# A signal of its own for the gate half of the products in the expert tiles

## What is computed

```python
x = x + tanh(g_xattn) * mlstm(layernorm(x), ctx, ctx)        # 16 heads, over 128 positions
h_in = layernorm(x)                                           # 1024 x 256
logits = 30 * tanh(h_in @ w_gate / 30)                        # 8 experts
weights = softmax(logits) * (one of the 2 largest)
for e in range(8):
    h = silu(h_in @ w1[e]) * (h_in @ w3[e])                   # 256 -> 512
    out += h @ w2[e] * weights[:, e:e+1]                      # 512 -> 256
x = x + tanh(g_ffn) * out
```

## Time and profile before

| | us |
|---|---|
| median of the 3 runs | 222.68 |
| lowest and highest run | 222.11, 222.68 |
| span of the profiled execution | 219.9 |
| PE busy in the span | 200.4 (91%) |
| VectorE (DVE) busy | 161.1 (73%) |
| ScalarE (ACT) busy | 140.4 (64%) |
| GpSimd (POOL) busy | 89.4 (41%) |

### The profile page before, as it was taken

One profiled execution on the slowest core, in us unless ns is written; L12 is line 12 of the kernel. 1 busy time (PEld: TensorE's weight loads), 2 busy tenths in 40 slices (PEclk: granted clock), 3 DMA queues, 4 the chain that ended last, 5 costly groups with the idle time before them and its releaser, 6 DMA issues.

```text
span 219.9 us, 4347 instructions
## 1 busy us (share of the span) xinstructions
PE 200.4 (91%) x1373; PEld 142.2 (65%) x1374; DVE 161.1 (73%) x354; ACT 140.4 (64%) x281; POOL 89.4 (41%) x96
## 2 busy tenths in 40 slices
PE   8999899989889898979999999999999999999930
PEld 3478554434346544468888888888888888888720
DVE  6897764688989889998777747767767777667520
ACT  2387878898964797746666645566566665665510
POOL 8100254338380000611555555555444555532232
PEclk9999999999999999999999999999999999999996
DMA  3999999921010124110222332334333233342212
GB/s 110 322 366 375 372 375 372 373 88 48 3 48 3 48 87 156 48 51 24 51 48 48 51 48 48 52 51 67 56 54 60 48 48 48 53 62 33 24 24 24
DMA packets 20034, 23.43 MB, mean 107 GB/s; under 512 B 3888, under 2 KB 15152, under 8 KB 20016
## 3 DMA queue, kind: packets, MB, share of 16 engines
q1 hardware_dynamic: 13696, 16.94, 22.4%
q0 software_dynamic: 4464, 6.16, 17.1%
q10 hardware_dynamic: 1856, 0.10, 0.6%
HBM read 17.95 MB, written 5.24 MB: 105 GB/s over the span
## 4 chain that ended last, share of the span: by engine, by line
PE 67%; DVE 16%; ACT 6%; DMA 4%; issue 3%; POOL 1%; DVEq 0%; ACTq 0%; POOLq 0%
PE bank L1446 28%; PE bank L1258 7%; PE bank L1466 6%; PE bank L1478 6%; PE bank L1457 5%; PE bank L1298 3%; PE bank L1469 3%; DMA x_sb<-in_x_dram 3%; ACT arena L511 2%; PE bank L1428 2%; DVE w_sb_r L973 2%; DMA out_dram<-hraw,sidx 2%; PE bank L1274 2%; PE bank L1179 1%; DVE st L801 1%
## 5 line engine op out<-in xcount | busy, mean ns | idle before, releaser
L1446 PE MATMUL bank<-arena_r,xn_sb_r 128*128 x176 | 54.6, 391 | 0.0
L471 POOL DMA_INDIRECT out_dram<-hraw,sidx x16 | 26.1, 1632 | 38.5 <-DVE hraw L1135 22.5
L1446 PEld LDWEIGHTS bank<-arena_r,xn_sb_r 128*128 128x128 f32 x176 | 33.1, 188 | 6.7
L1446 PE MATMUL bank<-w_sb_r,xn_sb_r 128*128 x88 | 36.5, 415 | 0.3 <-issue 0.2
L676 ACT ACTIVATE x_sb<-bank 128x512 f32<-128x512 f32 x23 | 13.8, 599 | 29.7 <-PE bank L1446 26.4
L432 POOL TENSOR_SCALAR_AFFINE_SELECT arena<-arena 128x1024 f32<-128x1024 f32 x16 | 17.6, 1102 | 36.5 <-ACT arena L541 36.5
L1086 DVE TENSOR_TENSOR x_sb<-x_sb,bank 128x512 f32<-128x512 f32 x23 | 15.8, 686 | 16.4 <-ACT x_sb L676 16.4
L1162 PE MATMUL bank<-ones_b 128*128 128x512 bf16 x103 | 25.6, 397 | 1.1 <-POOL ones_b L385 1.1
L454 POOL DMA_INDIRECT cvT<-xnorm_scratch,gidx x12 | 12.3, 1028 | 31.2 <-DVE gidx L1035 23.4
L851 DVE TENSOR_TENSOR arena<-bank,arena 128x1024 f32<-128x1024 f32 x16 | 19.5, 1222 | 6.8 <-POOL arena L432 6.6
L973 DVE TENSOR_TENSOR w_sb_r<-w_sb,arena_r 128x512 fp32r<-128x512 f32 x32 | 20.1, 683 | 0.1
(11 more groups left out here) (234 smaller groups left out, 403.9 us busy)
## 6 DMA issues: line engine op xcount, KB each, us to landing
w_sb<-in_L_ffn_w_dram SPq DMA_DIRECT2D x24, 512.0 KB, 9.4
x_sb<-in_x_dram SPq DMA_DIRECT2D x2, 512.0 KB, 6.7
arena<-in_ctx_dram SPq DMA_DIRECT2D x2, 512.0 KB, 9.3
out_dram<-x_sb SPq DMA_DIRECT2D x8, 128.0 KB, 1.8
xnorm_scratch<-xn_sb SPq DMA_DIRECT2D x8, 128.0 KB, 1.9
out_dram<-hraw,sidx POOLq DMA_INDIRECT x16, 3.8
cvT<-xnorm_scratch,gidx POOLq DMA_INDIRECT x12, 2.8
hraw<-xnorm_scratch,gidx POOLq DMA_INDIRECT x11, 2.8
```

The costliest lines, as they stand in the source:

```text
L471: nc.gpsimd.indirect_dma_start(out=out[:, :], out_offset=bass.IndirectOffsetOnAxis(ap=sidx[:, i:i + 1], axis=0), in_=y_sb[i % YBUF], in_of ...
L1446: last = nc.tensor.matmul(ps_scores[p][:, n, :], a, w, start=(k == 0 and j == 0), stop=(k == KC - 1 and j == 2))
```

## The change

The signal `s_gu` becomes two. `s_gt` is raised by the last matmul of the gate half, `s_gu` by the last of the up half, as before. `silu` waits for `s_gt` alone; `hidden` waits for the SiLU and for `s_gu`. In `first_gate_up` the signals stand at the last gate and the last up matmul of its second part. No instruction is added, removed or moved on any engine: what differs is which semaphore an instruction raises or waits for, 23 more signals on PE and one more condition on each of the 23 `hidden` instructions.

```diff
-        s_gu = sem("gate_up_done")
+        s_gt = sem("gate_done")
+        s_gu = sem("gate_and_up_done")
...
             def silu(i, p):
-                act.wait_ge(s_gu, i + 1)
+                act.wait_ge(s_gt, i + 1)
...
             def hidden(i, p):
                 dve.wait_ge(s_si, i + 1)
+                dve.wait_ge(s_gu, i + 1)
                 nc.vector.tensor_tensor(h_sb[p], sg_sb[p], ps_scores[p][:, 1, :], ALU.mult).then_inc(s_hm, 1)
...
             def gate_up(i, p, e, split=True):
...
                             last = nc.tensor.matmul(ps_scores[p][:, n, :], a, w, start=(k == 0 and j == 0),
                                                     stop=(k == KC - 1 and j == 2))
-                last.then_inc(s_gu, 1)
+                    last.then_inc((s_gt, s_gu)[n], 1)
...
             def first_gate_up():
...
                                                         stop=(lower == 1 and k == KC - 1), skip_group_check=True)
-                last.then_inc(s_gu, 1)
+                        if lower:
+                            last.then_inc((s_gt, s_gu)[n], 1)
```

## The result

| | before | changed |
|---|---|---|
| median of 11 runs, us | 222.09 | 220.88 |
| lowest run, us | 221.79 | 220.50 |
| span of the profiled execution, us | 219.9 | 218.7 |

The changed kernel takes 0.9942 of the time before (95% interval 0.9928 to 0.9957): 1.2 us less by the medians, 1.3 by the ratio. One run of each kernel, 224.39 and 224.44 us, lies far above the others; without them the medians are 222.05 and 220.87. The span fell by 1.2 us, from 219.9 to 218.7; 218.8 was forecast. The sum of the change was right, and the time it was taken from was not.

The account below looks back on a forecast made before the run. PE's chain was taken to bound the kernel; 0.8 us from the loop's gaps and 0.3 from the last step give 1.1 to 1.15 off 219.9, to 218.8. Plus 2.8 outside the span: 221.5 us, range 221.0 to 222.5.

Parts of the forecast that it names:

- What bounds: Expert tiles: the chain runs along PE alone, so only its standing still or its matmuls stretching can win or lose time.
- SiLU and `hidden` earlier: Step 9 into 10: SiLU starts near 142.02 instead of 142.99, `hidden` near 142.98, 0.64 us earlier, with 0.62 us margin.
- The 11 gaps: Before `turn_h` in steps 9 to 19: 0.07 to 0.08 us each vanish, 0.8 us less, bounds 0 and 0.9.
- The last step: Before `gate_up(22)`: the stall from a late register load behind `turn_h(21)` goes, 0.32 us less, bounds 0 and 0.36.
- The end: Last addition waits for the DMA of tile 21, not for tile 22: earlier `turn_h(22)` worth 0, at most 0.2 us.
- the start: `hidden(0)` starts when `split(1)` lets go of DVE, and steps 1 to 7 have no gap before `turn_h`: worth 0.
- the signals: Extra signals on PE and waits on DVE: 0, at most 0.01 us per signal and 0.2 us for 23.
- Signals that cost: Signals amid the twelve `gate_up` matmuls hold the next by up to 0.03 us: 0.6 us given back, 222.1; chance 0.08.
- a stretch by SiLU's reads: SiLU reading the gate bank stretches the up half's six matmuls; at 20 ns each 2.8 us, 224.3 in all; chance 0.05.
- The unmoved gap: The loop's gap is PE's own register work and stays; only the final step gains, 222.4 us; chance 0.14.
- a gain in the loop only: The register load before `gate_up(22)` may wait for the transposes, so that stall stays: 221.9 us; chance 0.10.
- idle that moves elsewhere: Nothing happens, as PE's idle moves, for one to the wait for `lower_x`: 222.6 us; chance 0.05.

Follow-up runs that it names:

- the loop alone: The changed kernel with SiLU waiting for the gate half alone only in tiles 8 to 18, elsewhere for the up half: 221.24 us, 0.9960 of the time before.
- tile 21 alone: The changed kernel with SiLU waiting for the gate half alone only in tile 21, elsewhere for the up half: 221.72 us, 0.9972 of the time before.
- its own experiment: The kernel before, with only the register load of the last tile's expert moved ahead of `turn_h(21)` on PE: 221.64 us, 0.9978 of the time before.
- the late SiLU: The kernel before, with SiLU of tiles 8 to 18 also waiting for the two transposes behind `gate_up`: 225.02 us, 1.0125 of the time before.

## Why the prediction was right, and where it was wrong

**What bounds.** Right: PE alone, and the two kinds of stall named from "issue" waits were all that the change touched on it. **SiLU and `hidden` earlier**: `hidden` at 142.99 for 142.98 forecast. SiLU started at 141.85, earlier than the 142.02 forecast: the step began 0.07 us sooner by the closed gap, and ACT's row of SiLU begins 0.09 us before that of `upper_w2` ends (140.79 + 1.15). The reserve is 0.55 us instead of 0.62. The hit on `hidden` to a hundredth was luck in part: everything stood 0.07 us sooner, and the product came 0.11 us behind the end of `gate_up` where 0.03 was reckoned with. The lead of SiLU over the end of `gate_up`, put at 0.97 us, was 0.93 by the prediction's own rows (142.95 less 142.02) and came out at 1.03.

**The 11 gaps.** 0.8 us forecast; 0.82 in the chain, and 0.9 to 1.0 by the runs of the loop alone. **The last step.** 0.32 forecast within 0 to 0.36; with steps 20 and 21 the chain has 0.40, and 0.34 with tile 21 alone. The cause given, the register load, is shown by its own experiment. **The end, the start, the signals.** 0 each, and so they came out, but for 0.10 us by which one addition landed later. "No instruction is added" was wrong by 23, at no cost that can be measured.

**The step that failed** is the last of the sum: "The median of the runs stands 2.8 us over that span, the lowest 2.2. Kept at 2.8, this gives 221.5 us." The profiled execution was taken for a typical one of the three runs, and all the difference for time outside the span (2.2 to 2.8 us, as the section on the time before has it too). The runs that list both show 1.7 to 1.8 us outside the span in every single one, before as changed (220.51 with a span of 218.7). So the execution with a span of 219.9 was one of about 221.7 us, faster than all eleven runs, and the three first lay high: their median is 222.68, that of the eleven 222.09. The span forecast, 218.8, and 1.8 outside would be 220.6 us, and the forecast difference, 1.15 us, taken from the median of the eleven 220.94, both close to the 220.88 measured. The range failed by the same term: its low end, 221.0, is the span forecast with the 2.2 us of the fastest of the three runs, when 1.8 was the true term.

**The rivals.** Signals that cost and a stretch by SiLU's reads are out: `gate_up` has 2.75 to 2.78 us with SiLU reading beside it, 2.75 to 2.79 before. The unmoved gap is out by the list of waits and by the late SiLU; a gain in the loop only, by the run of tile 21 alone; idle that moves elsewhere, by the chain, where PE has no new wait.

## What to carry to other kernels

On an engine that the profile shows busy all the time (PE for 49.05 us of the 49.05 in ten loop steps before) the gain can lie in gaps of 0.1 us at one place of each step: look for weight loads that wait for "issue" and compare their start with the end of the work that they depend on. A consumer that needs half of a product gets a signal at that half; it cost nothing here, and two tenths of a microsecond of lead were nearly all that counted. Register loads belong ahead of the waits, not behind them. And a time is forecast from the ratio to the runs, while the span of one execution is put beside the runs only once it is known what lies around it.

## What was not expected

- A register load behind a wait cost PE 0.3 to 0.5 us: 0.32 before `gate_up(22)`, which the prediction had, and 0.47 before `gate_up(1)` (4.99 less 4.52), which it did not look for. Ahead of the wait neither leaves any idle.
- A second condition on a DVE instruction counts as an instruction of its own (4370 against 4347), and cost nothing here.
- The additions to the output, 3.8 us to land in the median, took 4.0 to 5.0 one behind the other in some executions and set the end then. They are the next bound: 4.6 us at best for a step of 4.83 us.
